# First pair's output projection in fp32 from unsplit weights, and new orders of work in the first, second and last pair

## What is computed

```
x = x + fake_quant(layernorm(x)) @ fake_quant(ctx)           # quantised cross product
x = x + attention(layernorm(x))                              # 32 heads of 32, rotary, causal
        # qkv = h @ qkv_w + qkv_b;  softmax(q k^T) v;  ctx @ out_w + out_b
x = x + layernorm(x) @ W^T + bias + sum_e w_e (x A_e^T) B_e^T    # low-rank experts, rank 256 in all
```

## Time and profile before

| what | value |
| --- | --- |
| median of 3 runs | 671.78 us (670.38 to 671.81) |
| the profiled execution, its own time | 670.29 us |
| its span in the profile | 668.6 us |
| mean granted TensorE clock | 0.974 of full |
| TensorE busy | 611.0 us, 91% of the span |
| VectorE busy | 460.8 us, 69% |
| ScalarE busy | 298.3 us, 45% |
| DMA | 109.09 MB, mean 163 GB/s |

### The profile page before, as it was taken

The page is one execution under the profiler, slowest core; times in us unless marked ns, Lnnn a source line. Parts: engine busy times, 40 slices in busy tenths (PEclk is TensorE's granted clock), DMA queues, the critical chain, the costliest instruction groups (busy, mean ns, idle before and its releaser), DMA issues.

```text
span 668.6 us, 12862 instructions
## 1 busy us (share of the span) xinstructions
PE 611.0 (91%) x4880; PEld 308.2 (46%) x4880; DVE 460.8 (69%) x933; ACT 298.3 (45%) x374; POOL 7.6 (1%) x18
## 2 busy tenths in 40 slices
PE   0648967789999999999999999999999998999997
PEld 0224533335545554555455455545545554445453
DVE  8699984756854985587478548855674658876861
ACT  3997757266346445534653463465240233201010
POOL 1100000000000000000000000000000000000000
PEclk9869987889999999999999999999999999999999
DMA  8999973484147408612850673184212025033221
GB/s 317 388 387 401 331 263 119 137 259 149 65 166 250 149 0 273 229 63 93 280 175 17 220 239 106 36 291 144 95 63 95 1 92 193 1 110 111 78 95 47
DMA packets 38361, 109.09 MB, mean 163 GB/s; under 512 B 4026, under 2 KB 4282, under 8 KB 38336
## 3 DMA queue, kind: packets, MB, share of 16 engines
q1 hardware_dynamic: 36560, 104.35, 44.9%
q0 software_dynamic: 1344, 4.23, 1.8%
q10 hardware_dynamic: 432, 0.18, 0.1%
HBM read 100.35 MB, written 8.39 MB: 163 GB/s over the span
## 4 chain that ended last, share of the span: by engine, by line
PE 82%; DVE 13%; issue 2%; ACT 2%; DVEq 0%; ACTq 0%
PE dense L1068 16%; PE dense L1070 15%; PE dense L1069 15%; PE cross L1090 8%; PE turn L1058 6%; PE dense L1184 4%; PE dense L1185 4%; PE dense L1186 4%; PE score L1145 3%; PE score L1171 2%; DVE wq L743 2%; PE dense L1077 1%; PE score L1134 1%; PE cross L1211 1%; DVE xa L752 1%
## 5 line engine op out<-in xcount | busy, mean ns | idle before, releaser
L1068 PE MATMUL dense<-wq,xn_h 128*128 128x512 f16 x448 | 171.6, 383 | 2.0 <-DVE wq L743 2.0
L1069 PE MATMUL dense<-wq,xn_h 128*128 128x512 f16 x448 | 171.0, 382 | 0.0
L1070 PE MATMUL dense<-wq,xn_l 128*128 128x512 f16 x448 | 170.8, 381 | 0.0
L306 ACT ACTIVATE code<-raw,cst,qc 128x1024 uint8<-128x1024 f32 x77 | 94.5, 1238 | 25.6 <-DMA raw<-in_ctx 25.4
L1090 PE MATMUL cross<-code,q1t 128*128 128x512 f16 x256 | 75.7, 401 | 15.3 <-DVE xa L752 9.9
L1070 PEld LDWEIGHTS dense<-wq,xn_l 128*128 128x128 f16 x448 | 44.2, 99 | 53.8 <-issue 1.7
L1068 PEld LDWEIGHTS dense<-wq,xn_h 128*128 128x128 f16 x448 | 44.1, 98 | 48.1 <-DVE wq L743 3.6
L1069 PEld LDWEIGHTS dense<-wq,xn_h 128*128 128x128 f16 x448 | 44.2, 99 | 44.6 <-issue 1.7
L774 DVE TENSOR_REDUCE smx<-score 128x8 f32<-128x512 f32 x32 | 21.9, 686 | 53.9 <-PE score L1145 53.9
L306 ACT ACTIVATE code<-lnt,cst,qc 128x1024 uint8<-128x1024 f32 x35 | 43.3, 1237 | 21.0 <-DMA lnt<-in_ctx 20.4
L762 DVE TENSOR_TENSOR rope<-dense,cst 128x512 f32<-128x512 f32 x32 | 22.0, 689 | 42.6 <-PE dense L1070 42.6
(11 more groups left out here) (137 smaller groups left out, 860.8 us busy)
## 6 DMA issues: line engine op xcount, KB each, us to landing
raw<-in_ctx SPq DMA_DIRECT2D x77, 512.0 KB, 4.8
lnt<-in_ctx SPq DMA_DIRECT2D x35, 512.0 KB, 4.3
wq<-in_qkv_w SPq DMA_DIRECT2D x11, 512.0 KB, 12.9
wo<-in_qkv_w SPq DMA_DIRECT2D x10, 512.0 KB, 11.5
wo<-in_ctx SPq DMA_DIRECT2D x8, 512.0 KB, 8.8
wq<-in_ctx SPq DMA_DIRECT2D x8, 512.0 KB, 11.6
x_scratch<-xb SPq DMA_DIRECT2D x8, 512.0 KB, 3.0
wq<-x_scratch SPq DMA_DIRECT2D x8, 512.0 KB, 3.7
```

The costliest lines, as they stand in the source:

```text
L306: act.activation(low_bytes, src, ACT.Identity, scale=qc[:, 1:2], bias=z2).then_inc(s_u8, 1)
L1068: pe.matmul(bank[:, :], a_h[:, k, :], w_hi, start=(k == 0 and not started), stop=False)
L1069: pe.matmul(bank[:, :], a_h[:, k, :], w_lo, start=False, stop=False)
L1070: ins = pe.matmul(bank[:, :], a_l[:, k, :], w_hi, start=False, stop=(k == KC - 1))
```

## The change

1. **Projection of pair 0** (`project_whole`): out of `c_full` (fp32, scaled by CSC*WSC, written by ScalarE's `c_whole` in place of `c_high` and VectorE's `c_low`) and the fp32 output weights as they lie staged, one fp32 matmul of 128x128 by 128x512 for each k, 16 in all in place of 48 fp16 ones. The output weights are split later: tile 24 at the end of pair 0, tiles 25 to 31 within pair 1, which is now written out with `late=True`.
2. **Places.** RING goes from 8 to 6; a tile `spare` (128 x 1024 fp32) takes the room, as staging of tile 31 and later for one of the low-rank parts. Other staging places move, and with them the waits of `load_weight` and `weight_hi`.
3. **`cross_evac`** runs as two instructions of 64x1024 over both banks (now one tensor), not four of 64x512.
4. **Start:** the two fills run on GpSimd; `outb` is loaded after `norm2(0)`; two low parts (not three) precede `x_low(0, .)`, ScalarE makes five high parts (not seven) before `x_high(0, .)`, and `qkv(0, 0)` waits for half of `x_low` at a time.
5. **Orders** of pair 0 on all engines, of the quantising in each pair, of the loads, and of the tail.

```diff
-RAW, RING = 2, 8
+RAW, RING = 2, 6
@@ staged
-            if j < 2 * KC + 3:
-                return at_stage[:, j - 2 * KC, :, :]
-            if j < 2 * KC + 6:
-                return v_stage[j - 2 * KC + 2]
-            if j < W_ALL - 2:
-                return o_stage[j - 2 * KC - 6]
-            return q_stage if j == W_ALL - 2 else rope_stage
+            if j < 2 * KC + 5:
+                return v_stage[j - 2 * KC + 3]
+            if j < W_QKV:
+                return at_stage[:, j - 2 * KC - 5, :, :]
+            return o_stage[j - W_QKV + 1] if j < W_ALL - 1 else spare_stage
@@ ScalarE weight_hi
-                if 2 * KC <= j < 2 * KC + 5:
+                if 2 * KC <= j < 2 * KC + 3:
                     act.wait_ge(s_wlo, j - 2 * KC + 1)
-                elif j >= 2 * KC + 5:
-                    act.wait_ge(s_wlo, j - 1)
+                elif 2 * KC + 3 <= j < W_QKV:
+                    act.wait_ge(s_wlo, j - 2)
+                elif j > W_QKV:
+                    act.wait_ge(s_out, 2)
+                    act.wait_ge(s_wlo, j)
+            def c_whole(half):
+                act.wait_ge(s_pv, half + 1)
+                ms, cols = slice(4 * half, 4 * half + 4), slice(half * NT // 2, (half + 1) * NT // 2)
+                for b in range(2):
+                    act.activation(c_full[:, ms, b * SEQ:(b + 1) * SEQ], S[b][:, cols].rearrange("p (m t) -> p m t", t=SEQ),
+                                   ACT.Copy, scale=CSC * WSC).then_inc(s_cl, 1)
@@ ScalarE first_pair, new order
+                w(5..16) q0 w17 qk_evac0 q1 w18 q2 w19 qk_evac1 q3 w20 q4 w21 qk_evac2 w22 q5 w23 q6 q7 qk_evac3
+                exponent0 exponent1 q8 v_evac0 q9 p_evac0 q10 p_evac1 q11 exponent2 q12 exponent3 v_evac1 q13
+                c_whole(0) p_evac2 q14 p_evac3 q15 c_whole(1) w24 ...
@@ SyncE load_weight and order
-                elif j == 2 * KC + 1:
-                    sp.wait_ge(s_at, 4)
-                elif 2 * KC + 3 <= j < W_ALL - 2:
-                    sp.wait_ge(s_wlo, j - 13)
+                elif 2 * KC <= j < 2 * KC + 5:
+                    sp.wait_ge(s_wlo, j - 12)
+                elif j == 2 * KC + 6:
+                    sp.wait_ge(s_at, 4)
+                elif W_QKV <= j < W_ALL - 1:
+                    sp.wait_ge(s_wlo, j - 14)
-            for c in range(5):
+            for c in range(7):
                 load_chunk(1, c)
                 load_weight(17 + c)
...
+            for c in range(7, 11):
                 load_chunk(1, c)
+                load_weight(17 + c)
+            for c in range(11, CHUNKS):
+                load_chunk(1, c)
+            for j in range(28, W_ALL):
+                load_weight(j)
@@ GpSimd
+            pool.memset(bias_stage, 0.0).then_inc(s_bset, 1)
+            pool.memset(code[:, :, :].rearrange("p r n -> p (r n)").bitcast(F32), CODE_PAIR).then_inc(s_fill, 1)
+            pool.wait_ge(s_xn, 1)
             pool.dma_start(outb[:, :], out_bias...)
@@ VectorE cross_evac
-                for n in range(2):
-                    dst = xa[rows, n * NT:(n + 1) * NT]
-                    link(dve.scalar_tensor_tensor(dst, X[n][0:SEQ, :], qc[0:SEQ, 2:3], dst, ALU.mult, ALU.add))
-                    dve.scalar_tensor_tensor(dst, X[n][SEQ:P, :], qc[SEQ:P, 2:3], dst, ALU.mult, ALU.add).then_inc(s_ce, 1)
+                link(dve.scalar_tensor_tensor(xa[rows, :], XX[0:SEQ, :], qc[0:SEQ, 2:3], xa[rows, :], ALU.mult, ALU.add))
+                dve.scalar_tensor_tensor(xa[rows, :], XX[SEQ:P, :], qc[SEQ:P, 2:3], xa[rows, :], ALU.mult, ALU.add).then_inc(s_ce, 1)
@@ VectorE first_pair (w: weight_lo, end exclusive)
-                w(3, 9)
+                w(2, 9)
                 rotate(0, 0)
-                out_base(0)
                 w(9, 13)
                 rotate(0, 1)
-                w(13, 17)
+                w(13, 16)
+                out_base(0)
                 rotate(0, 2)
-                w(17, 21)
+                w(16, 20)
                 rotate(0, 3)
-                w(21, 24)
+                w(20, 24)
                 softmax_in(0, 0)
...
-                w(24, 27)
+                cross_evac(1, 0)
                 softmax_in(0, 2)
                 softmax_in(0, 3)
-                cross_evac(1, 0)
                 softmax_out(0, 2)
                 softmax_out(0, 3)
-                w(27, 28)
-                c_low(0, 0)
-                w(28, 32)
-                c_low(0, 1)
                 cross_evac(1, 1)
                 norm2(1)
+                row_stats(2, x_early)
                 x_low(1, 0)
                 x_low(1, 1)
                 out_evac(0, 0)
+                w(24, 25)
                 out_evac(0, 1)
-                row_stats(2, x_early)
@@ VectorE next_pair(1, True, late=True): w25 behind row_codes, w26 behind rotate 0, w27 behind x_shift,
@@ w28 and w29 behind rotate 1, w30 behind softmax_out 1, w31 behind cross_evac(2, 0) and ahead of row_stats(3)
@@ ScalarE next_pair, new order of every pair (w only in pair 1)
+                w25 q2 q3 q4 a_high a_high w26 q5 q6 w27 qk_evac0 q7 q8 w28 qk_evac1 q9 w29 q10 q11 w30 exponent0 q12
+                exponent1 q13 qk_evac2 p_evac0 p_evac1 qk_evac3 q14 w31 v_evac0 q15 exponent2 exponent3 c_high0 ...
@@ VectorE tail, new order
+            ... out_evac(7, 0) merged_low(6) merged_low(7) merged_sum(8) y_low(0, 0) merged_sum(9) merged_low(8)
+            out_evac(7, 1) merged(10, 11) residual(0, 0, 0) merged(12) stats3(1, 0) merged(13, 14, 15)
+            merged_low(15) apply3(1, 1) residual(1, 1, 0)
@@ TensorE
+            def project_whole(n, half, between={}):
+                if half == 0:
+                    pe.wait_ge(s_v, n + 1)
+                if n == 0:
+                    pe.wait_ge(s_cl, 2 * half + 2)
+                for k in range(4 * half, 4 * half + 4):
+                    if n == 0:
+                        pe.wait_ge(s_w[W_QKV + k], 16)
+                    ins = pe.matmul(D[n][:, :], c_full[:, k, :], staged(W_QKV + k)[:, n, :], start=(k == 0), stop=(k == KC - 1))
...
+                qkv(0, 3, {1: [at(c, 1)], 3: [at(c, 2)], 5: [at(turned, 0, 0), at(qk_turn, 0, 2)], 7: [at(c, 3)]})
+                qkv(0, 4, {1: [at(c, 4)], 2: [at(scores, 0, 0)], 4: [at(c, 5)], 5: [at(turned, 0, 1), at(qk_turn, 0, 3)], 6: [at(c, 6)]}, tiles_due(2 * KC))
+                qkv(0, 5, {0: [at(c, 7)], 1: [at(turned, 0, 2), at(p_turn, 0, 0)], 2: [at(scores, 0, 1)], 3: [at(p_turn, 0, 1)], 6: [at(c, 8)], 7: [at(c, 9)]})
                 values_due(0, 0)
+                c(10)
                 values(0, 0)
+                project_whole(0, 0, {0: [at(evacuated, 0, 0), at(p_turn, 0, 2)], 1: [at(c, 11)], 2: [at(evacuated, 0, 1), at(p_turn, 0, 3)], 3: [at(c, 12, 13)]})
                 c(14, 15)
+                project_whole(1, 0, {2: [at(values_due, 0, 1)], 3: [at(values, 0, 1)]})
+                project_whole(0, 1, {7: [at(x_turn, 1)]})
+                project_whole(1, 1)
```

More of the change, by code:

```diff
@@ L144, in build @@
         S = [es.enter_context(nc.psum_tensor(f"score{n}", [P, NT], F32)) for n in range(2)]
-        X = [es.enter_context(nc.psum_tensor(f"cross{n}", [P, NT], F32)) for n in range(2)]
+        XX = es.enter_context(nc.psum_tensor("cross", [P, 2 * NT], F32))
+        X = [XX[:, n * NT:(n + 1) * NT] for n in range(2)]
         s_scal = sem("s_scal")
@@ L368, in q @@
                         quantise(1, c)
-                w(*range(7, 17))
+                w(*range(5, 17))
                 q(0)
@@ L376, in first_pair @@
                 w(19)
+                qk_evac(0, 1)
                 q(3)
-                qk_evac(0, 1)
                 w(20)
@@ L415, in first_pair, with next_pair @@
                 x_high(1, 1)
-            def next_pair(i, more):
+            def next_pair(i, more, late=False):
                 def q(*cs):
@@ L420, in q, with w @@
                         quantise(i + 1, c)
+                def w(j):
+                    if late:
+                        weight_hi(j)
+                w(25)
                 q(2, 3, 4)
@@ L423, in next_pair @@
                 a_high(i + 1, 1)
[L424 removed]
+                w(26)
+                q(5, 6)
+                w(27)
                 qk_evac(i, 0)
[L426 removed]
+                q(7, 8)
+                w(28)
                 qk_evac(i, 1)
[L428 removed]
+                q(9)
+                w(29)
+                q(10, 11)
+                w(30)
                 exponent(i, 0)
+                q(12)
+                exponent(i, 1)
                 q(13)
[L431 removed]
                 qk_evac(i, 2)
[L433 removed]
                 p_evac(i, 0)
                 p_evac(i, 1)
+                qk_evac(i, 3)
+                q(14)
+                w(31)
+                v_evac(i, 0)
                 q(15)
[L437 to L438 removed]
                 exponent(i, 2)
@@ L484, in _ @@
             a_high(1, 1)
-            for j in range(7):
+            for j in range(5):
                 weight_hi(j)
@@ L489, in _ @@
             first_pair()
```

(45 more changed lines are left out.)

125 lines of the change are left out of this document (40 added, 85 removed).

## The result

The changed kernel takes 655.22 us (median of 4 runs, 654.06 to 656.15) beside 671.1 us for the kernel before (4 runs, 670.38 to 671.81). The ratio is 0.9763, with a 95% interval of 0.9741 to 0.9784: 15.9 us faster. Forecast were 653.0 us and a range of 646 to 663.

What follows compares the result with a forecast made beforehand. VectorE's and ScalarE's lists, with the splitting of 8 output tiles, were taken to bound 82 to 137.1 us. Terms -19.5 + 2.3 - 0.8 = -18.0 gave 652.3 for the profiled execution; 653 was taken, range 646 to 663.

Steps and rivals of the forecast that it cites:

- start of pair 0's `qkv`: Start: fills off VectorE, merged evacuation and fewer low parts let pair 0's `qkv` start at 41.75, 3.6 us earlier.
- given back up to product 5: Q, K, V of pair 0: VectorE's low parts hold TensorE, so 1.15 of the 3.6 us is lost again.
- product 5 to projection: Pair 0 up to the projection: chunk 8's wait goes, `c_whole(0)` is late; the step shrinks from 27.9 to 13.9, 14.0 us.
- projection: Pair 0's projection to pair 1's start: 16 fp32 products at 0.853 us; the step goes from 19.3 to 19.7 us.
- rest of pair 1: Pair 1: tile 31's high part behind q14 delays VectorE and then TensorE; cost 2.3 us, bounds 0 and 3.8.
- tail: End of kernel: `merged_sum(8)` moved up saves a wait, `merge(15)` waits about 2.4; net 0.8 us gained, bounds -1.5 and +3.
- rival B: Start: GpSimd's fill is slow; 655 us at 3 times VectorE's time, 662 at 5 times; chance 0.05.
- One sign of being wrong: Before pair 0's projection: DMA waits of ScalarE over 3 us from 70 to 95 us would show the forecast wrong.
- Rival C: Projection: fp32 matmuls cost 1.7 us each, 666 us in all (0.05), or beyond 2.06, slower than before (0.03).
- 0.8 + 2.1: Before the projection: 0.8 us charged for `weight_hi(19)` waiting for tile 16's low part, 2.1 for `c_whole(0)` behind q13.
- rival A: Pair 0: waits move to ScalarE and SyncE's queue, or the clock halves; 5 to 9 us return, 657 to 662; chance 0.22.
- pair time of 59.1 us: Later pairs: a sign of being right was that pairs 2 to 6 take 59.1 us each.

Runs made afterwards that it cites:

- The reordered list: Changed kernel with ScalarE's exponents 2 and 3 ahead of q11 and `c_whole(0)` ahead of q12 and q13 in pair 0: 650.73 us, ratio 0.9691 to the kernel before.

## Why the prediction was right, and where its terms were off

The forecast was 653.0 us; the time is 655.22. The mechanism is the forecast one: the lists of VectorE and ScalarE bound 82 to 137 us, and taking the splitting out of pair 0, together with an earlier start, takes most of the idle time away. Term by term, gains positive, from the starts in the two traces (block 6 of pair 1 is the first matmul behind the turn of pair 2's codes):

| term | forecast | measured |
| --- | --- | --- |
| start of pair 0's `qkv` | 3.6 | 4.6 (45.74 to 41.13) |
| given back up to product 5 | -1.15 | -1.4 (82.04 to 78.84: 3.2 left) |
| product 5 to projection | 14.0 | 11.6 (27.8 less 16.2) |
| projection | -0.4 | -2.0 (19.4 to 21.4) |
| codes of pair 2 | 3.4 | 3.4 (7.9 to 4.5) |
| block 6 of pair 1 in all | 19.5 | 16.2 |
| rest of pair 1 | -2.3 | -2.0 (57.7 to 59.6) |
| pairs 2 to 7 | 0 | 0.9 |
| tail | 0.8 | 0.3 |
| span | 18.0 | 15.4 |

Three of the forecast's own figures don't follow from its working. 652.3 for the profiled execution and 1.5 for the median give 653.8, not 653, and the result is 1.4 us above that; between the profiled executions 15.4 us were gained of the forecast 18.0. The terms of the tail (1.7 less 0.4, less 2.4, and 0.7 and 1.0) add to 0.6, not 0.8. And rival B was priced for a fill of 4096 elements, where the ring of six places has 3072.

Of the signs, the 32 records of the fp32 products, chunk 8 without its wait and the wait before `values` in pair 1 came true; pair 1's first bias matmul came 3.4 us after the 113 that was named. One sign of being wrong came true in the sum: ScalarE waits 4.6 us for loads from 70 to 95 us (0.82, 1.22 and 2.53). It pointed at the term that was sized too small, the wait before the projection. The granted clock from 80 to 115 us was 0.95, so that sign did not show.

*Start.* 1 us better. Chunk 15 is quantised at 30.28 in place of the forecast 30.7, which is 0.4 of it; the rest is not traced to a term. The merged evacuation costs 1.27 and 1.29 us, as taken from the difference of two widths in the earlier trace rows. The loads did become the limit: ScalarE waited 0.2 us each for chunks 14 and 15. Rival B is out: GpSimd filled 3072 elements in 2.66 us and was done at 4.4, far under the 10.4 from which it would have counted. The rule of the Trainium skill, GPSIMD Engine Reference, Key points, by which GpSimd and VectorE contend for their shared interfaces, shows no effect here, and the trace does not test it. It speaks of VectorE instructions with two SBUF inputs or in a 2-port mode; beside GpSimd's fills VectorE ran only short fills and one of 0.91 us (1.60 to 2.51, as long as the same fill with GpSimd's two on VectorE), and then waited for a load until 5.07. So up to 4.4 us nothing ran that the rule names, and the hold-up that the forecast drew from it did not come.

*Q, K, V.* As forecast, with the new wait of `weight_hi(19)` (ScalarE resumes at 65.9, forecast 66.7).

*To the projection.* This is the term that was too large, by 2.4 us. The cause was named, and sized too small: a wait for `c_whole(0)` behind late chunks, forecast at 2.1 us and measured at 4.6. The prediction took the load of q13's chunk to be the late one; it was chunk 11's, with 8.44 us in flight, and on this list it held exponents 2 and 3 as well. The reordered list shows that this wait is ScalarE's order: it leaves 0.8 us. Chunk 8 does not wait for `cross_evac(1, 0)` (87.52), as forecast.

*Projection.* The price of an fp32 product of 512 columns, 0.853 us from two records of 0.427, holds: 0.86 to 0.88 between starts, 0.81 to 0.85 from doubling them. Rival C is out at either of its prices. Only the first product behind the long wait took 1.84. What was missed, 1.6 us, is mostly the half clock after the 4.6 us wait: about 1.0 on the first product, 0.4 on the turn and 0.1 on the next. With the short wait the step is 20.06, near the forecast 19.7. So the term that was mis-sized is "0.8 + 2.1" before the projection, which measured 5.2 (4.63 and 0.55 before a turn), and the miss behind it came with it; it is rival A in small (3.9 to 4.2 us, where it was given 5 to 9).

*Pair 1.* Tile 31 waits as forecast, and its cost against a steady pair is 3.8 us (64.16 and 60.3), the forecast's upper bound. Against the kernel before it is 2.0, because that kernel's own pair 1 was 1.7 us over a steady one from block 6 on; it began with matmuls at half clock behind its 2.6 us wait (137.13, 137.51, 137.94). So the near match of -2.3 and -2.0 is partly luck. The pair time of 59.1 us named among the signs was wrong as a number: a steady pair took 60.5 before and takes 60.3 now. No term rested on it.

*Pairs 2 to 7.* Forecast as nothing; the merged evacuation gives 0.18 us a pair, which the four-instruction version takes back in the trace.

*Tail.* Forecast to gain 1.3 at one place and lose 2.4 at another; the wait before merge 15 is 2.23, and the first one gone, but the sum is 0.3. Moving `stats3` behind the merges shows that this wait was the order's own. In some executions it cost the clock too, but not in the changed kernel's two.

That the number came out near owes something to offsets: the start and the later pairs gave 1.9 us more than forecast, the stage around the projection 4.0 less and the tail 0.5 less.

Left open: where the larger part of the merged evacuation's 4.0 us lies, whether the old tail costs anything (-1.1 to 3.5 with both intervals), what `row_stats(2)` moved by itself is worth, and how the gain would divide with lists made for each half of the change.

## What to carry to other kernels

When work leaves an engine's list, the next limit is often the order of the other engine's list: look for short instructions that stand behind one that waits for a transfer, and do not price the transfer by its median where the DMA engines are nearly full (8.44 us beside a median of 4.3 here). A wait of over 2 us before a run of matmuls costs its own length and, in about half of the executions or more, 1 to 2 us of half clock behind it, so two terms of a calendar hang on one lateness. A piece of work that is moved is free only where the engine that waits for what stands behind it has work of its own in that time; else it hands its lateness on, as `row_stats(2)` did to pair 1's first product in the kernel before.
